# Sharing the copy of an expert's weights between VectorE and ScalarE in the first 24 blocks of a mixture-of-experts stage

## The reference, cut to what matters

```python
def _L0_ffn_ref(x, w12, w3, gate_w):            # E = 8 experts, H = 512, D = 256
    scores = jnp.einsum('btd,ed->bte', x, gate_w)
    topk_scores, topk_idx = jax.lax.top_k(scores, 2)
    topk_probs = jax.nn.softmax(topk_scores, axis=-1)
    ...
    h12 = jnp.einsum('btd,ehd->bteh', x, w12)   # w12: (8, 1024, 256)
    h1, h2 = (h12[..., :H], h12[..., H:])
    hidden = jax.nn.silu(h1) * h2
    expert_out = jnp.einsum('bteh,edh->bted', hidden, w3)
    y = jnp.sum(total_probs[..., None] * expert_out, axis=-2)
```

## Time and profile before

| what | value |
|---|---|
| median of 3 runs | 633.19 us (631.81 to 634.0) |
| the profiled execution | 635.4 us, of it 633.7 us span |
| TensorE matmul busy | 547.5 us (86%) |
| VectorE busy | 485.1 us (77%) |
| ScalarE busy | 377.8 us (60%) |
| GpSimd busy | 329.0 us (52%) |
| copies to `w_of_block`, L1232 | 71, 86.8 us, 1223 ns each |
| stage of the blocks | about 115 to 416 us of the span |

### The profile page before, as it was taken

The page is one execution under the profiler, slowest core; times in us unless marked ns, Lnnn a source line. Parts: engine busy times, 40 slices in busy tenths (PEclk is TensorE's granted clock), DMA queues, the critical chain, the costliest instruction groups (busy, mean ns, idle before and its releaser), DMA issues.

```text
span 633.7 us, 17617 instructions
## 1 busy us (share of the span) xinstructions
PE 547.5 (86%) x5888; PEld 469.6 (74%) x5888; DVE 485.1 (77%) x1378; ACT 377.8 (60%) x690; POOL 329.0 (52%) x558
## 2 busy tenths in 40 slices
PE   5898875798898999999999999924777776999996
PEld 5787764788797899999999999913666543666665
DVE  5898879789788888767676666517777487999986
ACT  2378964356766654444444444414659948999994
POOL 2045554005403778888634334343556277978655
PEclk9856665799999999999999999975999999999999
DMA  8999851566552469898655555658674300011112
GB/s 316 359 369 417 308 170 53 151 162 185 177 137 63 143 98 97 100 102 101 92 69 69 69 70 68 110 128 313 228 281 127 99 1 1 26 43 43 43 42 76
DMA packets 88956, 87.21 MB, mean 138 GB/s; under 512 B 54179, under 2 KB 73507, under 8 KB 87846
## 3 DMA queue, kind: packets, MB, share of 16 engines
q1 hardware_dynamic: 75574, 68.26, 35.7%
q0 software_dynamic: 13296, 17.83, 17.7%
HBM read 44.35 MB, written 32.41 MB: 121 GB/s over the span
## 4 chain that ended last, share of the span: by engine, by line
PE 55%; DVE 17%; issue 9%; DMA 7%; ACT 7%; SPq 2%; POOL 2%; DVEq 1%; ACTq 0%; POOLq 0%
PE banks L790 20%; PE banks L803 10%; PE banks L1901 4%; PE banks L1877 4%; PE banks L744 2%; DMA expert_rows_in<-rows_of_tokens 2%; PE banks L723 2%; DMA w_slots<-in_w 2%; PE banks L733 2%; PE banks L1880 2%; DVE hidden_T L1240 2%; PE banks L1891 2%; PE banks L1810 1%; DMA z_parts<-in_ctx_rows 1%; PE banks L1817 1%
## 5 line engine op out<-in xcount | busy, mean ns | idle before, releaser
L790 PE MATMUL banks<-z_turned,w_of_block 128*128 128x128 f16 x3408 | 203.9, 221 | 2.9 <-DVE w_of_block L1232 2.4
L790 PEld LDWEIGHTS banks<-z_turned,w_of_block 128*128 128x128 f16 x3408 | 197.9, 98 | 6.2 <-DVE w_of_block L1232 3.1
L589 POOL DMA_INDIRECT rows_of_tokens<-x_rows,row_tokens x71 | 119.7, 1685 | 79.0 <-ACT x_rows L668 53.4
L581 POOL DMA_INDIRECT z_rows<-z_parts,places_in_regions x64 | 74.9, 1170 | 142.5 <-DVE z_parts L1008 95.1
L659 ACT ACTIVATE hidden_T_high<-hidden_T 128x512 f16<-128x512 f32 x71 | 44.8, 631 | 130.6 <-PE banks L803 81.7
L803 PE MATMUL banks<-w_slots,hidden_T_high 128*128 x568 | 99.5, 273 | 10.2 <-DVE w_of_block L1232 9.8
L1240 DVE SCALAR_TENSOR_TENSOR hidden_T<-banks,blk_scales,silu_T 128x512 f32<-128x512 f32 x71 | 53.2, 749 | 68.0 <-PE banks L790 53.8
L1232 DVE COPY w_of_block<-w_slots 128x4096 f16 x71 | 86.8, 1223 | 2.0 <-issue 0.8
L803 PE MATMUL banks<-w_slots,hidden_T_low 128*128 x284 | 77.5, 273 | 0.0
L803 PEld LDWEIGHTS banks<-w_slots,hidden_T_high 128*128 128x128 f16 x568 | 52.6, 98 | 19.5 <-issue 14.7
L652 ACT ACTIVATE silu_T<-banks,blk_scales 128x512 f32<-128x512 f32 x71 | 48.4, 682 | 19.1 <-PE banks L790 19.1
(11 more groups left out here) (299 smaller groups left out, 1113.5 us busy)
## 6 DMA issues: line engine op xcount, KB each, us to landing
w_of_block<-in_ctx_and_x_turned SPq DMA_DIRECT2D x16, 512.0 KB, 6.4
w_slots<-in_w SPq DMA_DIRECT2D x8, 1024.0 KB, 9.5
x_rows<-in_x SPq DMA_DIRECT2D x8, 512.0 KB, 8.3
w_slots<-in_w SPq DMA_DIRECT2D x8, 512.0 KB, 11.2
rows_of_tokens<-x_rows SPq DMA_DIRECT2D x8, 512.0 KB, 4.1
rows_of_tokens<-zero_rows SPq DMA_DIRECT2D x8, 512.0 KB
z_parts<-in_ctx_rows SPq DMA_DIRECT2D x16, 256.0 KB, 3.7
x_rows<-rows_of_tokens SPq DMA_DIRECT2D x8, 512.0 KB, 8.6
```

Of the source, the lines that this page charges most:

```text
L581: pool.indirect_dma_start(z_rows[:, :], bass.IndirectOffsetOnAxis(ap=put_at[:, t, k:k + 1], axis=0), zp[:, t % ZP, :], None).then_inc(scat ...
L589: pool.indirect_dma_start(token_rows[:, :], bass.IndirectOffsetOnAxis(ap=dest[:, j:j + 1], axis=0), X1[:, j % T, :], None, compute_op=ALU. ...
L790: mm = pe.matmul(up_bank(j, half)[:, hc * P:(hc + 1) * P], win[:, u, wp, c, at:at + P], zturn[:, j % ZB, k, :], start=(n == 0), stop=(n == ...
```

## The change

In blocks 3 to 23, the copy is made by two engines. VectorE copies the first three quarters (3072 of 4096 values on each partition), and ScalarE the last quarter (the low part of the second chunk, 1024 values), with an ACTIVATE of its own, `hold_rest`. ScalarE issues hold_rest(j+3) in step j, for j = 0 to 20, behind round_g(j+1) and ahead of keep_y(j-1). It waits for the same `w_low` count as the copy of VectorE does. ScalarE also loads the experts of the blocks into registers now: once before its first silu, and in steps 5 and 13 ahead of hold_rest. TensorE waits for both parts. From block 24 on the copy is whole, as it was.

```diff
+SHARED = 24
...
+            def hold_rest(j, u, e):
+                act.wait_ge(w_low, 3 * min(E, max(j - 1, 0) // 4 + 1))
+                act.wait_ge(h2_made, j - 1)
+                a.activation(win[:, u, 1, 1, :], W12[:, e, 1, 1, :].rearrange("p b h -> p (b h)"),
+                             ACT.Copy).then_inc(yg_made, 1)
...
             act.wait_ge(tables, TABLE1)
+            e = [bass.ds(n, 1) for n in block_values(mybir.EngineType.Activation, blk_slot, 0, E)]
             silu(0, 0)
             round_g(0, 0)
...
                     silu(j + 1, 1 - u)
                     round_g(j + 1, 1 - u)
+                if (j + 3) % READ == 0 and j + 3 < SHARED:
+                    e = [bass.ds(n, 1) for n in block_values(mybir.EngineType.Activation, blk_slot, j + 3, E)]
+                if j + 3 < SHARED:
+                    hold_rest(j + 3, 1 - u, e[(j + 3) % READ])
                 if j:
                     keep_y(j - 1, 1 - u)
...
                     pe.wait_ge(win_made, j + 1)
+                    if 3 <= j < SHARED:
+                        pe.wait_ge(yg_made, T // 2 + j - 2)
...
-                v.tensor_copy(win[:, u, :, :, :].rearrange("p a c h -> p (a c h)"),
-                              W12[:, bass.ds(e[j % READ], 1), :, :, :].rearrange("p b a c h -> p (b a c h)")).then_inc(win_made, 1)
+                n = (3 if 3 <= j < SHARED else 4) * 2 * H
+                v.tensor_copy(win[:, u, :, :, :].rearrange("p a c h -> p (a c h)")[:, 0:n],
+                              W12[:, bass.ds(e[j % READ], 1), :, :, :].rearrange("p b a c h -> p (b a c h)")[:, 0:n]).then_inc(win_made, 1)
```

## The result

| | before | after |
|---|---|---|
| median | 633.6 us (631.81 to 634.34, 4 runs) | 647.92 us (646.37 to 649.6, 4 runs) |
| span of the profiled execution | 633.7 us | 645.6 us |
| H(1) to H(21), steps 0 to 19 | 92.20 us | 103.98 us |
| TensorE's waits for VectorE's copy behind L803 (L818 after) | 9.8 us, 11 times | 17.4 us, 15 times |

The change made the kernel slower: the ratio is 1.0218, with a 95% interval of 1.0182 to 1.0253 (whether by a full 2%, these runs leave open).

The account below looks back on a forecast made before the run. The longer of ScalarE's and VectorE's queues sets each step from H(n), the start of hidden(n), to H(n+1). Steps 0 to 19 grow 11.7 us, the way to up(24) 0.5: 633.2 + 12.2 = 645.4 us, range 641 to 649.

Parts of the forecast that it names:

- (a): VectorE's copy loses a quarter: 0.27 us shorter each, counting only in steps that VectorE still sets.
- (b): ScalarE's 21 passes over 1024 values, between round_g and the next silu: 1.06 us long alone, 0.96 each in the queue.
- (c): In steps 2, 6, 10, 14, 18 hold_rest waits for VectorE's low part: 0.84, 0.65, 0.78, 0.75, 0.73 us.
- (d): ScalarE's register loads in steps 5 and 13, partly hidden under round_g: up to 0.42 us shows, 0.35 taken twice.
- TensorE's second wait: TensorE's extra wait for ScalarE's part (`yg_made`): costs nothing of itself, as VectorE still copies when hold_rest ends.
- The sum: H(1) to H(21), starts of hidden(1) and hidden(21): 92.20 to 103.89 us; then up(24) 7.95 after H(21), another 0.5.
- From the stage to the time: The end moves by 12.2 us: profiled execution 635.4 to 647.6 us, median 2.2 lower, 645.4 us.
- (1): Rival: copy was late because it was long; 13 VectorE-set steps gain 0.27 each, 3.5 us, 629.7 us; chance 0.05.
- (2): Rival: ScalarE's pass is cheap, 0.53 us as over 512 values; +5, 638 us; chance 0.06.
- (3): Rival: TensorE's clock falls; two blocks of about 8 us in steps 3 and 4 cost 4.1 us, 649.5 us; chance 0.07.
- (4): Rival: the delay is absorbed later, where TensorE is busy 164.68 of 165 us; within 0.3% of before; chance 0.02.
- The signs named ahead: TensorE's stage waits up from 9.8 to about 22 us; wrong if ScalarE-set steps don't grow 0.96 or gaps beyond 240 us.

Follow-up runs that it names:

- dve_alone: Kernel before, VectorE copying only 3072 of 4096 values in blocks 3 to 23 and nobody copying the last quarter: 631.24 us, ratio 0.9958.
- pass_later: Changed kernel with ScalarE's pass and its register loads put behind keep_y and the late tile, ahead of high_w: 644.11 us, ratio 1.0165 to before.
- again: The changed kernel run once more, unaltered, beside the kernel before on one chip: 647.29 us, ratio 1.0211.
- act_alone: Changed kernel, but VectorE copies all 4096 values and ScalarE's pass writes to a place nobody reads: 647.65 us, ratio 1.0210 to before.
- eighth: Changed kernel, but ScalarE copies an eighth (512 values) and VectorE seven eighths: 639.68 us, ratio 1.0090 to before.
- tail_share: The change's edit in blocks 24 to 70 in place of 3 to 23, 47 passes: 635.60 us, ratio 1.0027 to before.
- in_gap: Changed kernel with ScalarE's pass between silu(j+1) and round_g(j+1), in 16 blocks only: 633.50 us, ratio 0.9979 to before.
- high_in_gap: Kernel before, no shared copy, with high_w moved between silu(j+1) and round_g(j+1): 625.93 us, ratio 0.9862.
- both_in_gap: Kernel before with high_w and, in steps 0, 1, 5, 9, 13, 17, ScalarE's quarter copy between silu and round_g: 625.70 us, ratio 0.9859.

## Why the prediction was right, point by point

- **What bounds the stage.** That the interval of two hiddens is the longer of two queues gave the steps of the kernel after within 0.04 us, but for steps 5, 6, 8 and 13 (see the sum). Of the kernel after, steps 3, 4, 7, 9, 11, 15, 16 and 19 were 6.34, 5.48, 6.33, 6.40, 5.33, 6.34, 5.47 and 5.34 us; each grew by 0.93 to 0.96.
- **(a) VectorE's copy.** 0.27 a copy was right (1.22 to 0.95), and dve_alone gives 3.2 us over the steps 0 to 19.
- **(b) ScalarE's pass.** Forecast 1.06 long and 0.96 in the queue, measured 1.04 and 0.94 to 0.95. The Trainium skill's 186 ns + 0.833 ns an element ("ScalarE: Activation LUTs", "What ACT_TABLE_LOAD costs") gives 1.04 for 1024 values and 0.61 for 512; the runs have 1041 and 614 ns.
- **(c) The new wait.** 0.65 to 0.84 a step forecast, 3.75 over the five. The profile's brackets have 3.5 us; counted as in the forecast, from 1.38 us after hidden to the start of the pass, it is 0.69 to 0.87 a step and 3.9 in all. By pass_later, 2.30 us of it were on the path in steps 2, 6, 10 and 18.
- **(d) The register loads.** 0.35 each was a little high for the kernel after. In its step 5 round_g starts at 149.09 and hold_rest at 149.85, 0.76 later and not 0.53 or 0.54. But it isn't a constant: in step 13 of the run `again` the pass started 1.65 us after round_g, 1.1 us more than without a load and 0.9 more than in the same step of the kernel after, and this alone is its 0.9 us more. The same place shows 0.45 us in step 5 of act_alone, and 0.35 and 0.50 in steps 5 and 13 of eighth. The profile names TensorE's L805 as the releaser, but the up whose end this pass waits for is the one that hidden(14) had needed already, so I take it for the load; no run tells it apart. The two rows, of `again`:

```profile
190.41 0.63 ACT L660 ACTIVATE hidden_T_high<-hidden_T 128x512 f16<-128x512 f32 x1 [0.93 <-DVE hidden_T L1256]
192.06 1.06 ACT L666 ACTIVATE w_of_block<-w_slots 128x1024 f16 x1 [1.01 <-PE banks L805]
```

- **TensorE's second wait.** The prediction let it cost nothing of itself, since VectorE would still be copying when hold_rest ends. That is wrong in the steps without a low part (3, 7, 11, 15 and 19), where the pass ends 0.6 to 0.8 us behind the copy. In step 3 of the kernel after, VectorE's copy ends at 138.22 and ScalarE's pass at 138.84 (its row stands above), and TensorE starts again 0.20 us behind the pass, after 0.28 us of idle time. The profile does not name the releaser ("issue"); I read it from the ends, and in steps 15 and 19 TensorE also starts 0.20 to 0.21 us behind the pass.

```profile
137.27 0.95 DVE L1248 COPY w_of_block<-w_slots 128x3072 f16 x1
```

```profile
139.04 0.28 PE L818 MATMUL banks<-w_slots,hidden_T_high 128*128 x1 [0.28 <-issue]
```

It did not lengthen these steps: they are 6.34, 6.34 and 5.34 us, what ScalarE's queue alone comes to (6.36, 6.36 and 5.36).

- **The sum.** 103.89 us forecast from H(1) to H(21), 103.98 measured; 7.95 from H(21) to up(24), 7.97 measured. The errors of single steps (step 5 4.69 for 4.81, step 13 4.68 for 4.81, step 8 4.76 for 4.50, step 6 5.27 for 5.11) cancel, so that the total is this close is in part luck. The 0.26 us of step 8 I can't explain: round_g starts 1.12 or 1.13 us after hidden there and not 0.85, in all five profiles with the pass behind round_g, and in none of the others.
- **From the stage to the time.** The forecast was 12.2 us; the profiled executions give 12.6 and 13.4 in the stage and the two sets of runs 14.3 and 13.6 (2.11% of 633.66 is 13.4), with an interval that begins at 11.3 (0.0179 x 633.66). So 12.2 lies inside. Of the 12.6, 11.8 lie ahead of H(21), 0.5 up to up(24), and 0.26 behind it, where the gap at 247.84 us is; the 0.9 us more in `again` are its step 13. What the medians have beyond that is not explained. The profiled execution was forecast at 647.6 us and took 647.3, but this too is partly luck: its H(1) came 1.57 us earlier than before (123.06 for 124.63; in all the runs it lies between 121.84 and 124.82), and what follows the blocks took 0.9 us more. And the 2.2 us by which the forecast put the median below the profiled execution were scatter: after the change the median lies 0.6 us above it. What follows the blocks shows no clear part of it, since from their last matmul to the end the profiled executions of all the runs take 216.8 to 220.1 us with no order in them (before 217.8, after 218.7, again 220.1, act_alone 217.5).
- **The rivals.** (1), the copy was late because it was long: dve_alone (7.5 of the 9.8 us of waits left) and the 17.4 us of waits rule it out as the main cause. (2), a cheap pass: 1041 ns. (3), the clock: it did fall, once behind H(1) in the kernel after, but without lengthening a step. Two windows and the timeline of TensorE, kernel after:

```profile
143.00:146.00 3.00, 0.41 (x4) 0.20 (x3) 3.00 (x6) 2.39 (x4) 0.00 (x0) 1.00 0.39 88
148.00:150.00 2.00, 2.00 (x22) 2.00 (x21) 1.76 (x2) 0.94 (x3) 1.34 (x2) 0.51 0.18 67
```

```profile
145.79 0.28 PE L818 MATMUL banks<-w_slots,hidden_T_high 128*128 x1 [2.59 <-DVE w_of_block L1248]
146.02 4.47 PE L805 MATMUL banks<-z_turned,w_of_block 128*128 128x128 f16 x48
```

TensorE stood for 2.59 us, and the 48 matmuls of the next block took 4.47 us instead of 2.84, the granted clock being 0.51 (1.2 GHz) for most of it. The steps then under way, 4 and 5, were 5.48 and 4.69 us, which is what ScalarE's queue alone comes to (5.50, and 2.50 + 1.00 + 0.96 + 0.22 for the load = 4.68): TensorE had room to be slow in. `again` shows the same without a sum: the clock fell a second time there, from 178 to 184 us, and its steps 10 to 12 are 4.27, 5.34 and 4.49 us, where the kernel after, with no dip there, has 4.28, 5.33 and 4.49. In the kernel before, all windows from H(1) to the end of the blocks stood at 1.00. The profiles of act_alone, pass_later and eighth have such dips too, and dve_alone, tail_share, in_gap, high_in_gap and both_in_gap have none behind H(1). The price that the prediction set, two whole blocks at about 8 us, did not come up either.
- (4), absorbed later: the stretch from 262 us on has as little idle time as before.
- **The signs named ahead.** Two came out otherwise. TensorE's waits were to go up to about 22 us. The view that had 9.8 has 17.4; all of TensorE's idle time from H(1) to the end of the blocks went from 10.8 to 20.4 us, and the rest of the stage's 12.6 us is 2.9 us more of busy time, in part from the slow clock. And the prediction was to be wrong if TensorE had gaps beyond 240 us: it has one, of 0.22 us at 247.84, and `again` has it too (0.21). That sum let TensorE run without a gap from up(24) on, which is off by this much.

## What to carry to other kernels

When two engines hand work to each other and back in every step, find the point where their queues meet, and add up each queue from there to the next meeting; a busy share of 60% says nothing about whether there is room. Idle time can be used only by what stands in the queue ahead of the wait: the same 1.04 us pass cost 0.96 us behind the wait in every step that ScalarE set, and nothing ahead of it. And a piece of work moved from one engine to another is worth its length only in the steps that the first one sets, and costs its length in those that the second one sets; here VectorE set 13 of the 21 steps, with 0.27 us to gain in each, and the pass, at 0.96 us, made ScalarE the longer queue in ten of them, so that only steps 0, 1 and 14 gained.

## What the runs showed of the hardware

Loading eight register values on ScalarE between two passes showed 0.22 us in step 5 of the kernel after, and in step 13 of `again`, the same program, 1.1 us stood in the same place; that this is the load is inferred. TensorE's clock fell to 1.2 GHz behind a stand of 2.59 us in the kernel after, and did not fall behind one of 2.73 us 33 us later, nor from H(1) on in the kernel before, whose longest stand in the blocks was 1.92 us. In pass_later it fell behind a stand of 1.59 us, so the length of the last stand alone does not tell. Two engines that write parts of one buffer at the same time didn't slow each other: VectorE's short copy takes 946 ns at the least with ScalarE's pass in the same step, and 937 ns at the least without it (dve_alone), and ScalarE's pass takes 1.04 to 1.06 us in the kernel after and in in_gap. The five short copies of the kernel after that lie wholly inside a pass took 0.96 us. In tail_share 19 of the 47 short copies took 1.04 to 1.29 us, most of them with no more than 0.04 us of a pass beside them; what held them is not known.
